# A graph kernel on one core: how edge counts are applied to node features (bf16 pieces as the moving operand, or fp32 counts as the moving operand)

## The reference, cut to what matters

```python
def _graph_conv(h, src, dst, n, W_root, W_rel, b):
    agg = jax.ops.segment_sum(h[src], dst, num_segments=n)
    return h @ W_root.T + agg @ W_rel.T + b
...
h = jax.nn.relu(_graph_conv(x, src, dst, n, W1_root, W1_rel, b1))
out = jax.nn.relu(_graph_conv(h, src, dst, n, W2_root, W2_rel, b2))
```

## Time and profile before

| what | value |
| --- | --- |
| timed runs | 4912.16, 4938.74, 4939.9 us; median 4938.74 us |
| profiled execution | 4902.4 us, of which the span of its instructions 4900.6 us |
| mean granted TensorE clock | 0.887 of full speed |
| busy in the span | TensorE 3921.1 us (80%), its weight loads 3185.6 us, VectorE 3512.9 us (72%), ScalarE 2093.4 us (43%), GpSimd 905.6 us (18%) |
| device memory | 287.83 MB read, 110.03 MB written |

### The profile page before, as it was taken

How to read it: one execution, slowest core, us unless ns; L and a number is a source line. 1 busy time by engine, 2 the same in 40 slices (tenths; PEclk the granted TensorE clock), 3 DMA queues, 4 the chain that set the end, 5 groups by cost and what they waited for, 6 DMA issues and landing times.

```text
span 4900.6 us, 236239 instructions
## 1 busy us (share of the span) xinstructions
PE 3921.1 (80%) x108223; PEld 3185.6 (65%) x108223; DVE 3512.9 (72%) x4267; ACT 2093.4 (43%) x2437; POOL 905.6 (18%) x809
## 2 busy tenths in 40 slices
PE   5532957859368588888888886999999799999997
PEld 4531856848358466666666665997898566666665
DVE  5875676877758877777777766553554699999997
ACT  5201112010010477767667764662564245544453
POOL 0565757534422410000000000000000000000000
PEclk9975786959669799999999998997999699999998
DMA  6751443616225111111111113552553000000000
GB/s 159 246 142 30 117 139 84 183 58 174 63 63 171 47 53 54 53 54 53 47 54 53 54 51 100 178 179 79 171 177 125 5 10 11 10 10 11 10 11 17
DMA packets 208019, 404.97 MB, mean 83 GB/s; under 512 B 106418, under 2 KB 126132, under 8 KB 207268
## 3 DMA queue, kind: packets, MB, share of 16 engines
q1 hardware_dynamic: 181672, 383.04, 24.9%
q0 software_dynamic: 25472, 10.79, 1.1%
q10 hardware_dynamic: 184, 0.08, 0.0%
HBM read 287.83 MB, written 110.03 MB: 81 GB/s over the span
## 4 chain that ended last, share of the span: by engine, by line
PE 69%; DVE 11%; issue 7%; POOL 3%; ACT 3%; DMA 1%; DVEq 0%; ACTq 0%; SPq 0%
PE psum L1110 19%; PE psum L1083 15%; PE psum L1150 13%; PE psum L910 10%; PE psum L1071 4%; POOL heads_d L602 2%; PE psum L878 2%; POOL gath L610 1%; DVE space L1637 1%; PE psum L991 1%; PE psum L992 1%; PE psum L852 1%; ACT space L759 1%; PE psum L1159 1%; DVE space L1422 1%
## 5 line engine op out<-in xcount | busy, mean ns | idle before, releaser
L764 ACT COPY space<-psum 128x784 f32<-128x784 f32 x1184 | 966.1, 816 | 627.4 <-PE psum L1083 625.4
L1083 PE MATMUL psum<-space 64*128 64x49 bf16 x56832 | 986.7, 184 | 179.1 <-issue 149.1
L1083 PEld LDWEIGHTS psum<-space 64*128 64x128 bf16 x56832 | 851.6, 94 | 389.2 <-issue 279.1
L1110 PE MATMUL psum<-space,X 128*64 128x256 f32 x7252 | 1039.2, 396 | 14.8 <-issue 12.2
L1637 DVE TENSOR_TENSOR space<-space 128x2352 bf16<-128x2352 bf16 x592 | 814.3, 1376 | 0.0
L910 PE MATMUL psum<-table,space 128*128 128x56 bf16 x24300 | 674.8, 189 | 118.7 <-DVE space L1292 77.8
L910 PEld LDWEIGHTS psum<-table,space 128*128 128x128 fp8e4 x24300 | 660.7, 96 | 132.8 <-issue 116.6
L1631 DVE TENSOR_TENSOR space<-space,V 128x2048 bf16<-128x2048 bf16 x592 | 720.9, 1218 | 0.0
L1150 PE MATMUL psum<-space 128*128 128x192 bf16 x7252 | 627.3, 247 | 23.8 <-DVE space L1733 23.8
L1150 PEld LDWEIGHTS psum<-space 128*128 128x128 bf16 x7252 | 593.9, 98 | 49.4 <-issue 48.8
L1289 DVE TENSOR_REDUCE space<-psum 128x1512 f32 (+1 forms) x300 | 518.5, 1731 | 137.5 <-PE psum L910 132.6
(11 more groups left out here) (284 smaller groups left out, 2892.8 us busy)
## 6 DMA issues: line engine op xcount, KB each, us to landing
space<-adj_d SPq DMA_DIRECT2D x148, 784.0 KB, 4.2
space<-onehots SPq DMA_DIRECT2D x240, 432.0 KB
adj_d<-space SPq DMA_DIRECT2D x74, 784.0 KB, 3.6
onehots<-space SPq DMA_DIRECT2D x60, 432.0 KB, 3.2
space<-digit_rows SPq DMA_DIRECT2D x60, 378.0 KB
space<-cw_d SPq DMA_DIRECT2D x37, 160.0 KB, 2.3
cw_d<-space SPq DMA_DIRECT2D x4, 1184.0 KB, 13.3
heads_d<-spread,heads_at POOLq DMA_INDIRECT x280
```

The source lines that it names most:

```text
L764: nc.scalar.copy(A[:, h, :, b * P:(b + 1) * P].rearrange("p a (w s) -> p w a s", w=2)[:, :, :, c:c + UC], psum[:, 2 + 2 * (k % 2):4 + 2 * ...
L1083: mm = nc.tensor.matmul(psum[:, 2 + 2 * (k % 2) + w, c * NB:(c + 1) * NB], ohlo[lo:hi, ring, col // 2, :, col % 2], ohw[lo:hi, ring, r, co ...
L1110: mm = nc.tensor.matmul(pb[6][half:half + F, 0:2 * P], X[:, a, :], A[:, 1 - h, a, :], start=(a < 2), stop=(a >= NB - 2))
```

## The change

Blocks are applied in pairs. The counts are cast to fp32 into A, [128, 49, 256] for a pair, in four groups of chunks (CUTS: two groups by ScalarE, two by VectorE), with two buffers for A and two for the bytes. TensorE holds X (fp32, 64 columns) stationary and moves 256 columns of counts, as L1110 does; the pieces of X are gone. ScalarE copies out what is summed, a fold and the placing follow as in the weighted sums. The sums go to the upper 64 rows of xT, cleared by GpSimd, so that the products are one matmul of 128 rows a chunk with both weights below each other (`bothT`); the bias is added by VectorE. The first loads and casts of a pass stand ahead of its start in the queues. In the first weighted sum a block's counts are stored by four DMAs instead of one (STORES), each for a quarter of the chunks and one unit after the other, and the load of codes stands between the stores of the two blocks. "One tensor of 128 rows" is `bothT`, or xT with both halves.

```diff
+STORES = [(0, 13), (13, 25), (25, 37), (37, NB)]
+CUTS = [(0, 11), (11, 21), (21, 35), (35, NB)]
...
+            def store_counts(i, h, b, last=False):
+                for q, (lo, hi) in enumerate(STORES):
+                    sp.wait_ge(adj_made, i * (4 * GU) + ((2 * h + b + 1) * GU + (0 if last else q)))
+                    sp.sem_inc(sp_ok, 1)
+                    at = slice(...) if isinstance(i, int) else bass.ds(i * 4 + (2 * h + b), 1)
+                    sp.dma_start(adj_d[at, :, lo * P:hi * P].rearrange("b p x -> (b p) x"),
+                                 adj[:, b, lo:hi, :].rearrange("p a s -> p (a s)")).then_inc(adj_stored[b], 16)
...
SyncE, loads:
+            def load_pair(i, h, n):
+                for b in range(2):
+                    sp.dma_start(adj8[:, h, b, :, :], adj_d[at].rearrange("g p (a s) -> (g p) a s", s=P)).then_inc(adj_loaded[h], 16)
+            def first_loads(n):
+                for h in range(2):
+                    if n == 0:
+                        sp.wait_ge(adj_stored[h], 16 * len(STORES) * NDB)
+                        sp.wait_ge(at_read, NB // 7)
+                    else:
+                        sp.wait_ge(cast_act, 2 * NDB)
+                        sp.wait_ge(cast_dve, 2 * NDB)
+                    load_pair(0, h, n)
...
GpSimd:
-            nc.gpsimd.memset(xT[F:F + 1, :], 1.0).then_inc(ones_back, 1)
+            nc.gpsimd.memset(xT[F:P, :], 0.0).then_inc(acc_zero, 1)
+            pool.wait_ge(mm_psum, NMG)
+            nc.gpsimd.memset(xT[F:P, :], 0.0).then_inc(acc_zero, 1)
...
ScalarE:
+            def cast(n, i, h, parts=(0, 1)):
+                d = i * 2 + (n * NDB + h)
+                act.wait_ge(adj_loaded[h], ...)
+                for g in parts:
+                    lo, hi = CUTS[g]
+                    act.wait_ge(applied, d * 4 + (g + 1 - 8))
+                    nc.scalar.copy(A[:, h, lo:hi, :].rearrange("p a (b s) -> p b a s", b=2), adj8[:, h, :, lo:hi, :]).then_inc(cast_act, 1)
+            def apply_step(n, i, h, at):
+                D = i * 2 + (n * NDB + h)
+                if 1 <= at < NDB - 1:
+                    cast(n, i + h, 1 - h)
+                if 1 <= at <= NDB:
+                    act.wait_ge(applied, D * 4)
+                    if at >= 3:
+                        act.wait_ge(folded, D - 2)
+                    nc.scalar.copy(turned_sum[:, 1 - h, :], pb[1 - h][:, 0:2 * P]).then_inc(row_ready, 1)
+                if 2 <= at:
+                    act.wait_ge(folded, D - 1)
+                    if at >= 4:
+                        act.wait_ge(placed, D - 3)
+                    nc.scalar.copy(slots3[:, h, :, :], pb[2 + h][:, 0:2 * F].rearrange(...)).then_inc(slots_out, 1)
...
TensorE, products:
-                        nc.tensor.matmul(o, xT[0:F + 1, j * P:(j + 1) * P], weights, start=True, stop=False)
-                        mm = nc.tensor.matmul(o, acc[0:F, j * P:(j + 1) * P], more, start=False, stop=True)
+                        mm = nc.tensor.matmul(o, xT[:, j * P:(j + 1) * P], bothT[:, n, :], start=True, stop=True)
...
-                    for a in range(NB):
-                        mm = nc.tensor.matmul(pb[r % 2][:, 0:3 * F].rearrange("p (k f) -> p k f", k=3), adjb[:, r % 2, a * P:(a + 1) * P],
-                                              pieces[:, :, a * F:(a + 1) * F], start=(a == 0), stop=(a == NB - 1))
...
+            def apply_step(n, i, h, at):
+                D = i * 2 + (n * NDB + h)
+                if at < NDB:
+                    if n or at >= 2:
+                        pe.wait_ge(row_ready, D - 1)
+                    for g, (lo, hi) in enumerate(CUTS):
+                        pe.wait_ge(cast_act if g < 2 else cast_dve, D * 2 + (g % 2 + 1))
+                        for a in range(lo, hi):
+                            half = F * (a % 2)
+                            mm = nc.tensor.matmul(pb[h][half:half + F, 0:2 * P], X[:, a, :], A[:, h, a, :], start=(a < 2), stop=(a >= NB - 2))
+                        mm.then_inc(applied, 1)
+                        if g == 1 and at >= 2:
+                            place_slots(D, h, at)
+                        if g == 2 and at >= 1:
+                            fold_sum(D, h, at)
...
+            def place_slots(D, h, at):
+                pe.wait_ge(slots_out, D - 1)
+                pe.wait_ge(place_ready, D - 1)
...
+                    mm = nc.tensor.matmul(pb[4 + h][F:P, b * P:(b + 1) * P], slots3[:, h, b, :], place[:, h, b, :], start=True, stop=True)
+            def fold_sum(D, h, at):
+                pe.wait_ge(row_ready, D)
...
+                    mm = nc.tensor.matmul(pb[3 - h][:, b * F:(b + 1) * F], turned_sum[:, 1 - h, b * P:(b + 1) * P], fold[:, :], start=True, stop=True)
...
VectorE, after each pass:
-                        nc.vector.tensor_scalar(X[:, lo:hi, :], p, 0.0, None, ALU.max).then_inc(mm_read, 1)
+                    nc.vector.tensor_tensor(x, p, biases[:, u - 1, :]..., ALU.add).then_inc(mm_read, 1)
+                        link(nc.vector.tensor_scalar(x, x, 0.0, None, ALU.max))
```

More of the change, by code:

```diff
@@ L800, in _ @@
+            cast(0, 0, 0, parts=(0,))
+            root(0, NB)
+            cast(0, 0, 0, parts=(1,))
+            for n in range(2):
+                if n:
+                    cast(n, 0, 0)
+                    cast(n, 0, 1)
+                else:
+                    for h in range(2):
+                        act.wait_ge(adj_stored[h], 16 * len(STORES) * NDB)
+                copy_xt(0, NB)
                 if n == 0:
+                    cast(n, 0, 1)
+                for at in range(4):
+                    apply_step(n, at // 2, at % 2, at)
+                with act.Fori(2, NDB // 2) as i:
@@ L1172, in acc_rows @@
+            def blocks(n):
+                for at in range(4):
+                    apply_step(n, at // 2, at % 2, at)
+                with pe.Fori(2, NDB // 2) as i:
+                    for h in range(2):
+                        apply_step(n, i, h, 4)
+                for at in range(NDB - 1, NDB + 2):
+                    apply_step(n, at // 2, at % 2, at)
             def acc_rows(n):
@@ L1771, in _ @@
+                for part in range(2):
+                    bases = bases_at(2 * NDB - 8 + 4 * part, 4)
+                    for h in range(2):
+                        at = NDB - 1 + 2 * part + h
+                        apply_step(n, at // 2, at % 2, at, bases[2 * h:2 * h + 2])
+                dve.wait_ge(merged, 2 * (n + 1) * NDB)
+            cast(0, 0, 0)
+            cast(0, 0, 1)
             for u in (1, 2):
                 blocks(u - 1)
+                if u == 1:
+                    cast(1, 0, 0)
+                    cast(1, 0, 1)
```

219 lines of the change are left out of this document (100 added, 119 removed).

## The result

| what | before | after |
| --- | --- | --- |
| median of the runs | 4939.32 us | 4976.91 us (4968.74 to 4984.54) |
| profiled execution, its span | 4902.4 us, 4900.6 us | 4968.74 us, 4966.9 us |
| mean granted clock | 0.887 | 0.896 |

One of the four runs of before, at 10597.13 us, is not comparable with the rest and is left out of the ratio; without it the median of before is 4938.74 us. After to before is 1.0088, 95% interval [1.0049, 1.0127]. A repetition on another chip gave 1.0076 [1.0054, 1.0099].

The account below looks back on a forecast made before the run. TensorE alone was taken to bound the apply passes. Passes +233.1, starts -22.4, tails +1.6, products -58.8 and stores -40 us sum to +113.5 us, giving 5052 us (+2.3%), range 4982 to 5130 us.

Parts of the forecast that it names:

- The apply passes: Both fp32 apply passes: 12.2 us a pair of blocks, 902.8 us against 669.7 us, so +233.1 us.
- The place: Two placing matmuls in each pair of the apply passes: 0.44 us plus 0.1 us for a switch, 0.54 us.
- The waits: Added waits at a pair's start and ahead of chunk groups: 0.17 us each, two of four counted, 0.34 us a pair.
- Starts of the passes: From X ready to a pass's first product: dropping the split and casting early saves 11.2 us a pass.
- Products: Products behind each pass: 49 matmuls at 0.616 us, 30.2 us instead of 59.6 us, -29.4 us a pass.
- Stores: Counts' stores in the first weighted sum: quarter-size stores shorten TensorE's issue idles, -40 us, between 0 and 110 us.
- The base: Whole kernel: timed median 36 us above the profiled execution's 4902.4 us, a difference carried over to reach 5052 us.
- (4): Apply passes: fp32 stream runs faster than in the weighted sum; at 0.085 us a record, kernel 4874 us; chance 3%.
- (3): Apply passes: drains and waits at six borders a pair cost 0.17 us each, +67 us, kernel 5119 us; chance 13%.
- (1): First weighted sum: all stalls come from the stores and go, -110 us instead of -40, kernel 4982 us; chance 12%.
- (2): First weighted sum: splitting the stores brings nothing, kernel 5092 us; chance 13%.
- (5): Apply passes: casts or loads come late through queue order, a pair takes 14 us, kernel 5185 us; chance 5%.

Follow-up runs that it names:

- e6: Kernel before with four stores a block, moved code load and joined 128-row products, VectorE clearing the sums, passes still bf16: 4791.98 us against 4933.25, 0.9704.
- e11: The changed kernel, unchanged, run again on another chip: 4969.56 us against 4935.29 us for the kernel before, ratio 1.0076.
- e9: The changed kernel with the fold's stationary operand cut to 64 columns, leaving out the other 64 slots' sums: 4934.65 us.
- e5: Kernel before with its products reordered, six matmuls over 65 rows, then six over 64: 4902.92 us against 4933.25 us, ratio 0.9936.
- e2: The changed kernel with GpSimd's clearing of the sums delayed until the second pass's X is there: 5641.64 us, ratio 1.0101 to the kernel before.
- e8: The kernel before, unchanged, run once more for a reference profile on that chip: 4931.37 us.
- e7: Kernel before with only the counts' stores split in four a block, code load left behind both blocks' stores: 4887.18 us, ratio 0.9905.
- e10: The changed kernel with 128 moving columns instead of 256, applying only the first block of each pair: 4606.01 us.

## Why the prediction was wrong, point by point

**What bounds the kernel, right.** The passes are TensorE's alone, and their change decides the sign: +185.8 us of passes against all that is gained elsewhere. e6 isolates this: without the fp32 passes, and the dropped split and earlier loads that go with them, the change gives -141 us instead of +34 (e11).

**The apply passes: right in kind, two terms failed.** 12.2 us a pair were forecast, 11.53 measured, which is 2 x 37 x 0.67 = 50 us, the largest part of the miss. The records, the place, the fold and the waits were added up as if they all stood in one line. Term by term:

- The place: "0.44 us. For the switch ahead of it I add 0.1 us ...: 0.54 us". This step failed. The place runs in the upper half, which has one chunk less than the lower one, and its price is 0. The 0.1 us for a switch is not there either: place and stream both have 64 stationary columns.
- The waits: "I take two, 0.34 us", between bounds of 0 and 0.68. This step failed too: measured 0. The idle of 0.17 us that the earlier trace rows show at a block's border did not carry over to a stream of longer instructions, which the same paragraph named as the reason for the lower bound.
- The records, 98 x 0.1093 = 10.71 us forecast; measured 50 x 0.216 = 10.79 us, the longer half's. The row of the weighted sum did contain the overlap, as the prediction says.
- The fold, 0.59 us forecast. The same stretch measured 0.59 us, but 0.15 us more lie just ahead of it and behind it: 0.74 us.

Together -0.54 - 0.34 + 0.08 + 0.15 = -0.65 us. The small terms that were too low made up for some of the large ones that were too high, by luck. (The upper bound of a pair is 11.84 + 0.68 = 12.5 us by its own terms, not 12.6.)

e9 bears on the rule weighed in the prediction. The Trainium skill, TensorEngine Tiling (Array Packing), Key Properties, says that a change of tiling mode drains TensorE. The trace agrees in kind: about 0.3 us for the way in and out of the fold, 0.19 us for a change between 65 and 64 rows (e5). But most of that was already inside the 0.59 us of the earlier trace rows, as the prediction had it; 0.15 us more came, and not up to 0.54.

**Starts of the passes, right.** 11.2 us forecast; X ready to first product went from 21.07 to 10.18 and from 21.18 to 10.11 us. Nothing took the place of the split. The tail of a pass, from its last apply product's end to VectorE's last addition, grew by 1.7 us where 0.8 was forecast.

**Casts and loads, right.** ScalarE casts a pair in 2 x 2432 ns and VectorE in 2 x 2027 ns:

```profile
L1806 DVE CAST space<-space 128x3584 f32<-128x3584 uint8 x148 | 299.4, 2027 | 256.4 <-PE psum L1203 256.3
L825 ACT CAST space<-space 128x2816 f32<-128x2816 uint8 (+1 forms) x148 | 352.8, 2432 | 141.0 <-PE psum L1203 136.8
```

Both wait for TensorE, not TensorE for them. The fp32 output did not halve VectorE's rate (0.57 ns an element in both kernels). The loads bring 139 GB/s; the forecast of 129 took the longer pair and slightly fewer bytes.

**Products: right in direction, the working failed.** The step that failed here: "The weight load is of 128 columns either way and sets the spacing: from one L991 to the next L992 it is ... 0.61 us at the low clock". Two matmuls of different rows were read as the spacing of two matmuls. 0.19 us of it was the alternation of 65 and 64 rows, which the change removes together with the second matmul. 49 x 0.427 = 21 us, not 30.2: 9 us a pass more were gained. The rule on modes, which I had weighed at the fold only, speaks for a gain here; held against the earlier trace rows, where the rows change at every record group, it would have named the term.

**A collision that was not forecast.** "GpSimd's clearing of 64 rows runs beside the layer norm and beside the transposes." It does, but in after it starts 0.35 us ahead of VectorE's last large relu and holds it for 4.9 us, once, ahead of the second pass (e2). The Trainium skill, SBUF — State Buffer, section "SBUF: two separate sides", describes it: GpSimd and some VectorE operations share a pair of ports, whichever starts first keeps it, and the other blocks fully. The trace agrees: the relu ends 0.3 us behind the clear. The bias addition that had begun 0.38 us ahead of the clear took its usual 0.69 us, and no other began while the clear ran, so whether one can be held was not seen.

**Stores.** -40 us was forecast and -33.1 stand in the table; by one profile each on one chip, e8 to e7, it is -40.1 for the stores alone, and the moved load adds -9.3 (e6). The -40 is inside what the profiles allow for the stores (23 to 44 us), and the load, which the forecast counted at nothing, may be worth about 9; neither is known to better than the 20 us by which executions of the same stage differ. The mechanism was only half right: I tied 42 idles to stores and expected them to go; they stayed and became shorter. They are waits for instructions, which come with either size of store; of e8's 155.8 us of issue idles on the three lines of the stage 125.7 are still there in e7. Nor do the 30 us less of them make up all of the 40.

**The base, right.** The forecast was 113.5 us on top of the median of before, and the miss of 75 us is one of the terms. It doesn't show in full in the table, because the profiled execution of before was a short one, 36 us under its median, and that of after only 8. The first weighted sum of that execution takes 1313.9 us where e8's takes 1330.8, 17 us less; what lies ahead of it ends at 1636.6 us, where after has 1647.7, 11 us less. These 28 us are the whole difference between 66 us by the profiles and 38 us by the medians. Against e8 and e11 the first weighted sum, to the same last copy, gains 1347.8 - 1296.6 = 51.2 us, and the sum is 185.8 - 22.0 - 71.9 - 51.2 - 3.5 = +37.2 us. So the miss is 49 us in the passes, 13 in the products (18 by the products, less the collision of 5), 11 in the first weighted sum and 4 in what wasn't touched.

**The rivals.** None of the five came true as written. (4), a faster stream, is refuted: the halves already overlap in full in the stream of the earlier trace rows (two records every 0.216 us there too), the mean is 0.1072 against the 0.094 us that it needed, and the pair is shorter for the place and the waits, not for the records. (3) is refuted, no border of a group costs anything. (1) and (2) both are out by e7, whose median is 46 us below before, neither 110 nor 0. (5) did not come: TensorE never waits for a cast inside a pass. The range failed because its lower end was that of the stores alone, while three terms went the same way together: the pair fell below the 11.8 us that I had called its lower bound (it still held the place's 0.54 us), the products had one reading and no bounds, and the moved load had neither.

## What to carry to other kernels

A spacing between two instructions is a price only if the change keeps both neighbours: look at which shapes alternate in the row, and take the price from a run of equal ones. A mean spacing can hide two streams that run side by side: look at the starts of single records, and add up each half of the array by itself, since work in the shorter half is free. Ask of each moved or added GpSimd operation which VectorE operation between two buffers of SBUF it can meet, and not only whether it has time. And a change that joins several edits can hide a good one behind a bad one: here the stores with the moved code load, the joined products and the clearing taken off a pass's start (e6) are worth -141 us together, and the fp32 passes take that back and more (e11's median is 178 us above e6's, with medians of before 2 us apart).

## What the runs showed of the hardware that was not expected

- An fp32 matmul leaves two records, and on 64 stationary columns each takes two cycles of 2.4 GHz per moving column: 0.216 us for 256, 0.109 us for 128. Matmuls for the two halves of the output rows run at the same time, in full: two records every 0.216 us, a mean of 0.1072 us (0.109 and 0.0546 for 128).
- In such a stream work for the half with fewer chunks is free: two matmuls of 128 columns cost 0 beside 24 and 25 chunks (after), and set the length of the pair when the stream's own columns are halved (e10).
- At the lower clock level, 128 x 64 fp32 products on 128 rows take 0.427 us each; a change between 65 and 64 rows costs 0.19 us. Two fold matmuls with 128 stationary columns in a stream of 64 cost 0.74 us at the upper level, with 64 columns 0.23.
- A GpSimd clear of 5.43 us holds VectorE's relu from 0.43 to 5.37 us.
- In an unrolled stream TensorE waits for its instructions: every one of its 184 "issue" idles in the stage of e8, 155.8 us in all, ends 1.2 to 1.6 us behind the landing of a 16 KB packet of the instruction queue. With stores of a quarter of the size there are nearly as many (174 in e7), 125.7 us, the longest at L1083's line 1.7 us instead of 2.5.
